# An adaptive-norm block on one core: load order, first stage, two orders in the step, and the second norm's statistics on ACT

## What is computed

```python
mod = silu(c) @ wmod                      # six rows of 128 per batch: sa, ca, ga, sb, cb, gb
ga, gb = sign(g) * max(|g|, 0.25)         # gates
h = layernorm(x) * (1 + ca) + sa
x = x + ga * attention(h)                 # eight heads of 16; windows of 64 tokens
h = layernorm(x) * (1 + cb) + sb          # the second norm
x = x + gb * ffn(h)                       # h + sum over 8 experts, two of them chosen by h[:, 0]
```

## Time and profile before

| | us |
|---|---|
| median of 3 runs | 681.24 |
| lowest and highest of them | 678.41, 683.61 |
| the profiled execution | 681.11 |
| its span, first to last instruction | 679.1 |
| mean granted clock of PE, share of full speed | 0.992 |

### The profile page before, as it was taken

How to read it: one execution, slowest core, us unless ns; L and a number is a source line. 1 busy time by engine, 2 the same in 40 slices (tenths; PEclk the granted TensorE clock), 3 DMA queues, 4 the chain that set the end, 5 groups by cost and what they waited for, 6 DMA issues and landing times. The chain is left out here.

```text
span 679.1 us, 22873 instructions
## 1 busy us (share of the span) xinstructions
PE 611.4 (90%) x6166; PEld 434.0 (64%) x6166; DVE 589.1 (87%) x4900; ACT 514.4 (76%) x1574; POOL 444.5 (65%) x723
## 2 busy tenths in 40 slices
PE   3989898999999999999999999999999999999886
PEld 2544456667666776666666766676666666776554
DVE  4885679999899989999999999999999899989860
ACT  2897257877888778877888888778888888778652
POOL 3011337778677767777777777777787677767651
PEclk9999899999999999999999999999999999999899
DMA  6220000000000000000110000000010000001000
GB/s 212 80 79 5 15 19 20 23 23 27 26 28 27 26 25 27 26 25 23 27 27 28 25 27 27 27 23 25 25 28 27 26 26 28 26 22 29 13 13 16
DMA packets 41183, 21.23 MB, mean 31 GB/s; under 512 B 6040, under 2 KB 40544, under 8 KB 41056
## 3 DMA queue, kind: packets, MB, share of 16 engines
q1 hardware_dynamic: 41056, 19.77, 10.2%
HBM read 10.45 MB, written 4.19 MB: 22 GB/s over the span
## 5 line engine op out<-in xcount | busy, mean ns | idle before, releaser
L1003 DVE MAX8 top<-modn_all 128x8 f32<-128x32 f32 x2048 | 208.1, 178 | 6.8 <-DVE meet L1095 0.5
L1009 DVE MATCH_REPLACE8 modn_all<-top,modn_all 128x32 f32<-128x32 f32 x1024 | 166.8, 176 | 0.0
L516 POOL TENSOR_TENSOR wmod_sb<-key,meet 128x512 f32<-128x512 f32 x64 | 67.7, 1058 | 114.7 <-DVE meet L1095 114.7
L1009 DVE MATCH_VALUE_LOAD modn_all<-top,modn_all 128x8 f32 x1024 | 80.8, 79 | 0.0
L1260 PEld LDWEIGHTS psC<-vst,big 128*128 128x128 f32 x512 | 62.0, 191 | 17.5 <-issue 17.5
L787 ACT ACTIVATE psD<-key 128x256 f32<-128x256 f32 x64 | 24.9, 389 | 62.3 <-issue 60.9
L1260 PE MATMUL psC<-vst,big 128*128 128x68 f32 x512 | 70.8, 280 | 0.0
L587 POOL TENSOR_TENSOR big<-big,con 128x512 f32<-128x512 f32 x64 | 69.8, 1091 | 0.7 <-DVE big L1064 0.7
L1260 PE MATMUL psC<-vdif,big 128*128 128x68 f32 x512 | 67.6, 274 | 0.0
L1260 PEld LDWEIGHTS psC<-vdif,big 128*128 128x128 f32 x512 | 62.3, 192 | 0.0
L1281 PE MATMUL psW<-con,wmod_sb 128*128 128x128 f32 x256 | 42.0, 287 | 19.3 <-POOL wmod_sb L516 19.3
(11 more groups left out here) (216 smaller groups left out, 1615.3 us busy)
## 6 DMA issues: line engine op xcount, KB each, us to landing
tst<-qT_all SPq DMA_DIRECT2D x256, 17.0 KB
big<-in_x SPq DMA_DIRECT2D x16, 256.0 KB, 2.9
xs<-in_x SPq DMA_DIRECT2D x64, 64.0 KB, 1.9
out<-yo SPq DMA_DIRECT2D x64, 64.0 KB, 1.6
sst<-nst SPq DMA_DIRECT2D x128, 3.0 KB
tst<-nst SPq DMA_DIRECT2D x128, 2.0 KB
con<-in_consts SPq DMA_DIRECT2D x1, 582.5 KB, 6.9
wmod_sb<-in_wmod SPq DMA_DIRECT2D x1, 384.0 KB, 5.8
```

The source lines that it names most:

```text
L516: nc.gpsimd.tensor_tensor(diff.rearrange("p (h j) -> p h j", h=NH), key[:, k % 2].rearrange("p (h j) -> p h j", h=NH), meet[:, k % 2, :, N ...
L1003: last = v.max(top[:, u, h, where], low_high[:, u, h])
L1009: last = v.match_replace(low_high[:, u, h], top[:, u, h, 1:9], low_high[:, u, h], GONE)
```

## The change

1. *Loads.* SP issues c first, then the identity alone (a DMA of its own), tile 0, wmod, tile 1, the query weights, the rest of the constants, tiles 2 and 3. Waits are split to match.
2. *First stage.* DVE clears a tile `warm`, on which PE makes 14 matmuls before it has work. The silu goes ahead of the first tile's statistics, tile 0 is normalised ahead of mod's two additions. The rows of mod, the Hebbian tables and the gate sizes leave the place ahead of the loop and stand within it: at n = 4 to 6 on ACT, n = 5 to 7 on PE, n = 10 on DVE.
3. *Routing.* PE makes the logits in step -2 and not -3, with other numbers of clock matmuls. DVE's last ten instructions of the expert gates go behind d2 of chunk 0. ACT's logarithm, root and influence of chunk 0 go behind the outer distances of chunk 1.
4. *The step, PE.* The masks go ahead of the counts.
5. *The step, ACT.* The root goes behind the copy L803, and the influence still stands last.
6. *The second norm.* bn_stats and bn_aggr leave DVE, and the three small instructions leave the head of ACT's step. ACT takes the sum with the copy to x2 (an accumulator), negates and scales it to the mean, squares x2 minus the mean with a second sum, and makes logarithm and exponential of that, all behind the copy and ahead of hi.

The diff, cut to its core (moved blocks that stay as they were are shown by their first lines):

```diff
@@ sync
-            for n in range(2):
-                sync.dma_start(xp[:, n], xh[:, n]).then_inc(xp_in[n], 16)
             sync.dma_start(c_sb[:], cin).then_inc(c_in, 16)
-            sync.dma_start(wmod_sb[:], wmod).then_inc(c_in, 16)
-            sync.dma_start(con[:], consts).then_inc(con_in, 16)
+            sync.dma_start(ident, consts[:, C_ID:C_ID + P]).then_inc(ident_in, 16)
+            sync.dma_start(xp[:, 0], xh[:, 0]).then_inc(xp_in[0], 16)
+            sync.dma_start(wmod_sb[:], wmod).then_inc(wmod_in, 16)
+            sync.dma_start(xp[:, 1], xh[:, 1]).then_inc(xp_in[1], 16)
             sync.dma_start(encq_sb[:], encq).then_inc(wq_in, 16)
+            sync.dma_start(con[:, C_MASK:C_END], consts[:, C_MASK:C_END]).then_inc(con_in, 16)
             for n in range(2, 4):
@@ scalar, first stage
-            act.wait_ge(c_in, 32)
+            act.wait_ge(c_in, 16)
...
-            act.wait_ge(pmod_ready, 2)
-            for j in range(2):
-                nc.scalar.activation(modn[:, j * 384:(j + 1) * 384], psW[0:NB, j, 0:384], ACT.Copy).then_inc(modn_ready, 1)
             act.wait_ge(modT_ready, 2)
             act.wait_ge(con_in, 16)
+            def modulation(j):
+                act.wait_ge(pmod_ready, 2 + j)
+                nc.scalar.activation(modn[:, j * 384:(j + 1) * 384], psC[0:NB, 0:384], ACT.Copy).then_inc(modn_ready, 1)
+            def hebbian():
+                act.wait_ge(pheb_ready, 2)
...
             to_hT(0, 0)
-            act.wait_ge(pheb_ready, 2)
...
                     to_q(n0 + u, u)
+                    if n0 == 4 and u < 2:
+                        modulation(u)
+                    if n0 == 4 and u == 2:
+                        hebbian()
@@ scalar, steps
+            def logarithm(k):
+                act.wait_ge(xT_ready, k + 1)
+                need(act, w_ready, k - 1)
+                if k == 0:
+                    act.wait_ge(r0_pe, 3)
+                nc.scalar.activation(infl[:, k % 2], pXT, ACT.Ln, bias=bias[:, 1:2]).then_inc(ln_done, 1)
+            def root(k):
...
+                nc.scalar.activation(e, e, ACT.Exp, scale=0.5).then_inc(root_done, 1)
+            def influence(k):
...
+                nc.scalar.activation(e, e, ACT.Exp, scale=-1.0).then_inc(infl_ready, 1)
             def step(i):
-                k = i - 4
-                if there(k):
-                    s = k % 2
-                    act.wait_ge(mvc_ready, k + 1)
...
-                    nc.scalar.activation(lv_c[:], mv_c[:, s, 1:2], ACT.Ln, bias=bias[:, 0:1]).then_inc(lnc_done, 1)
-                    nc.scalar.activation(nm_c[:, s:s + 1], mv_c[:, s, 0:1], ACT.Copy, scale=-1.0).then_inc(nm_done, 1)
-                    act.wait_ge(lnc_done, k + 1)
-                    nc.scalar.activation(rs_c[:, s:s + 1], lv_c[:], ACT.Exp, scale=-0.5).then_inc(rs_done, 1)
...
                     nc.scalar.activation(key[:, k % 2].rearrange("p (h j) -> p h j", h=NH), pA, ACT.Relu).then_inc(outer_ready, 1)
+                    if k == 1:
+                        logarithm(0)
+                        root(0)
+                        influence(0)
...
                 k = i - 3
                 if there(k):
+                    s = k % 2
                     act.wait_ge(att_ready, k + 1)
                     need(act, y_ready, k - 1)
-                    nc.scalar.activation(x2[:, k % 2], pAtt, ACT.Copy).then_inc(x2_ready, 1)
+                    need(act, rs_done, k)
+                    nc.scalar.activation(x2[:, s], pAtt, ACT.Copy, accum_out=sum_c[:]).then_inc(x2_ready, 1)
+                    act.wait_ge(x2_ready, k + 1)
+                    nc.scalar.activation(nm_c[:, s:s + 1], sum_c[:], ACT.Copy, scale=-1.0 / D).then_inc(nm_done, 1)
+                    act.wait_ge(nm_done, k + 1)
+                    nc.scalar.activation(dev_c[:], x2[:, s], ACT.Square, bias=nm_c[:, s:s + 1],
+                                         accum_out=ssq_c[:]).then_inc(ssq_done, 1)
+                    act.wait_ge(ssq_done, k + 1)
+                    nc.scalar.activation(lv_c[:], ssq_c[:], ACT.Ln, bias=bias[:, 0:1], scale=1.0 / D).then_inc(lnc_done, 1)
+                    act.wait_ge(lnc_done, k + 1)
+                    nc.scalar.activation(rs_c[:, s:s + 1], lv_c[:], ACT.Exp, scale=-0.5).then_inc(rs_done, 1)
                 k = i + 1
                 if there(k):
...
                     nc.scalar.activation(pHi, high, ACT.Copy, scale=-1.0).then_inc(hi_ready, 1)
-                    e = infl[:, k % 2]
...
-                    nc.scalar.activation(e, e, ACT.Exp, scale=0.5).then_inc(root_done, 1)
+                    if k:
+                        logarithm(k)
                 if there(i):
...
                     nc.scalar.activation(pHigh, top[:, 1].rearrange("p h n -> p (h n)"), ACT.Copy,
                                          scale=-1.0).then_inc(high_done, 1)
+                k = i + 1
+                if there(k) and k:
+                    root(k)
...
-                if there(k):
-                    e = infl[:, k % 2]
-                    act.wait_ge(root_done, k + 1)
-                    nc.scalar.activation(e, e, ACT.Exp, scale=-1.0).then_inc(infl_ready, 1)
+                if there(k) and k:
+                    influence(k)
@@ vector
-            stats(0, 0)
+            v.memset(warm[:], 0.0).then_inc(warm_set, 1)
             dve.wait_ge(ec_ready, 1)
...
+            stats(0, 0)
             stats(1, 1)
+            normalise(0, 0)
             dve.wait_ge(modT_ready, 1)
...
-            normalise(0, 0)
             normalise(1, 1)
...
-            dve.wait_ge(modn_ready, 2)
-            gview = modn.rearrange("b (u v d) -> b u v d", u=2, v=3)[:, :, 2]
...
+                    if n == 10:
+                        gate_sizes()
...
+            def expert_gates():
+                link(v.tensor_reduce(s8[:, 16, 0:1], s8[:, 12], AX_X, ALU.add))
...
                     v.scalar_tensor_tensor(out=e, in0=pB, scalar=0.0, in1=e, op0=ALU.max, op1=ALU.min).then_inc(d2_ready, 1)
+                    if k == 0:
+                        expert_gates()
...
-                k = i - 3
-                if there(k):
-                    dve.wait_ge(x2_ready, k + 1)
-                    need(dve, mvc_ready, k)
-                    v.bn_stats(st_c[:], x2[:, k % 2]).then_inc(stc_ready, 1)
...
-                    v.bn_aggr(mv_c[:, k % 2], st_c[:]).then_inc(mvc_ready, 1)
@@ tensor
+            pe.wait_ge(warm_set, 1)
+            for n in range(14):
+                mm(psC[0:1, :], warm[:, 0:1], warm[:], start=True, stop=True)
             pe.wait_ge(sil_ready, 1)
+            pe.wait_ge(wmod_in, 16)
...
-            for j in range(2):
-                last = mm(psW[0:NB, j, 0:384], sil[:], wmod_sb[:, j * 384:(j + 1) * 384], start=True, stop=True)
-            last.then_inc(pmod_ready, 1)
-            pe.wait_ge(con_in, 16)
-            pe.wait_ge(wq_in, 16)
-            pe.wait_ge(modn_ready, 2)
+            pe.wait_ge(ident_in, 16)
...
+                    if n0 == 5 and u < 2:
+                        modulation(u)
+                    if n0 == 5 and u == 2:
+                        hebbian()
...
                     need(pe, n2_ready, k - 1)
+                    need(pe, nst_ready, k)
...
                 if i == -3:
                     routing_front()
-                    keep_clock(psC, PW, 6)
+                    keep_clock(psC, PW, 8)
+                if i == -2:
                     routing_logits()
-                if i == -2:
-                    keep_clock(psC, PW, 8)
+                    keep_clock(psC, PW, 4)
...
+                k = i + 2
+                if there(k):
+                    need(pe, d2_ready, k)
+                    if k == 1:
+                        pe.wait_ge(pair_done, 2)
+                    for r in range(NR):
+                        masks(r)
                 drained({NCH - 1: 3, NCH: 3}.get(i, 0))
                 k = i - 1
                 if there(k):
                     pe.wait_ge(f_ready, 2 * k + 2)
...
                     pe.wait_ge(rows_in[k % 2], ROWS_IN * (k // 2) + ROWS_IN)
-                    need(pe, d2_ready, k)
-                    if k == 1:
-                        pe.wait_ge(pair_done, 2)
-                    for r in range(NR):
-                        masks(r)
                     last = distances(k % 2)
```

More of the change, by code:

```diff
@@ L858, in every_8th, with gate_sizes @@
                                 AX_X, ALU.add).then_inc(qsum8_ready, 1)
-            stats(0, 0)
+            def gate_sizes():
+                dve.wait_ge(modn_ready, 2)
+                gview = modn.rearrange("b (u v d) -> b u v d", u=2, v=3)[:, :, 2]
+                link(v.tensor_scalar(gsgn, gview, 0.0, 2.0, ALU.is_ge, ALU.mult))
+                link(v.tensor_scalar(gabs, gview, -1.0, None, ALU.mult))
+                link(v.tensor_tensor(gabs, gabs, gview, ALU.max))
+                link(v.tensor_scalar(gabs, gabs, 0.25, None, ALU.max))
```

(21 more changed lines are left out.)

76 lines of the change are left out of this document (41 added, 35 removed).

## The result

The changed kernel takes 695.23 us (median of 4 runs, 690.37 to 696.91) beside 680.50 for the kernel before on the same chip, so it is 14.7 us slower by the medians; the ratio of the means is 1.020, 95% interval 1.0135 to 1.0267. The forecast was 689, "same" or "slower" at equal chances. The profiled execution took 694.36 with a span of 692.5, 13.4 longer than before.

| stretch | before | after | measured | forecast |
|---|---|---|---|---|
| start to first scan | 92.52 | 98.81 | +6.29 | -2.6 |
| first scan to the scan of chunk 2 | 17.24 | 16.85 | -0.39 | -0.3 |
| 58 steps, chunk 2 to chunk 60 | 517.72 | 526.98 | +9.26 | +11.2 |
| last three steps | 27.84 | 27.08 | -0.76 | +0.9 |
| behind the last scan | 23.76 | 22.76 | -1.00 | -1.5 |

What follows compares the result with a forecast made beforehand. A ring of waits through DVE, POOL, PE and ACT, no single full engine, bounded the kernel. Terms 11.2 - 0.3 + 0.9 - 1.6 - 1.0 - 1.5 = +7.7 on 681.24 gave 689 us, range 677 to 701.

Steps and rivals of the forecast that it cites:

- +11.2: The 58 steps from chunk 2 to chunk 60: 528.9 us instead of 517.72, with plain steps of 9.03 instead of 8.63.
- -1.6: Loads and first stage: earlier third normalisation gains 2.9, moved gate sizes take back about 1.3; bounds -4 to +1.5.
- the forecast's own branch: Case where the step's ring of waits runs through masks and ACT's statistics: 683 to 695 us, chance 0.50.
- The chain: ACT's five dependent statistics activations between x2 and its negated copy: 1.56 us, bounds 1.25 to 1.92.
- The masks fill no gap: PE in each step: masks start only when d2 ends, so counts and all behind them move 0.68 later.
- the 1.5 expected: Tail behind the last scan: shorter x2 to n_c saves 1.0, the last chunk 0.5, so -1.5 us.
- Routing -1.0: Routing before the first scan: later expert gates gain some 0.4, the late root 0.6; bounds -2.5 to +0.5.
- The last three: +0.9: Last three steps: 0.9 us longer, including +0.4 for each of the two that contain ACT's negated copy.
- rival 3: Steps: ACT's statistics take 1.92, or PE's clock drops; 711 us, with half of it 700; chance 0.15.
- The scan still waits for L803, by about 0.9: Sign of being right, in a plain step: DVE's scan still waits about 0.9 us for ACT's copy.
- rival 2: Steps: DVE was the limit, so a step falls to 7.92 at best; 634 us, with half 657; chance 0.10.
- the 8.37 behind the late root: Plain step with the root moved later: 8.37 instead of 8.63, without DVE's idle 0.26, DVE then the limit.

Runs made afterwards that it cites:

- u_stats: Changed kernel with the second norm's statistics back on DVE, masks still ahead and root late: 662.52 us, ratio 0.972.
- best_dve: u_stats_ins plus the 14 clock matmuls of a_fill: 653.41 us, ratio 0.957.
- best_split: Front of u_stats_ins, clock matmuls of a_fill, and masks and statistics placed as in u_masks_split: 650.86 us, ratio 0.953.
- b_rm: Kernel before with masks ahead of the counts and root behind the copy L803, statistics on DVE: 655.78 us, ratio 0.963.
- b_root: Kernel before with only the root moved behind the copy L803: 662.27 us, ratio 0.970.
- b_masks: Kernel before with only the masks moved ahead of the counts: 683.97 us, ratio 1.006.
- u_stats_ins: u_stats with mod's rows, Hebbian tables and gate sizes put back ahead of the first stage's loop: 655.48 us, ratio 0.960.
- u_steps: Changed kernel with masks, root and second-norm statistics put back as before, leaving new loads, first stage and routing: 685.86 us, ratio 1.0043.
- a_fill: Changed kernel with 14 more PE clock matmuls in step -1, ahead of the turn of the expert gates: 692.75 us, ratio 1.014.
- u_masks: Changed kernel with only the masks put back behind the attention's product: 664.51 us, ratio 0.974.
- b_stats: Kernel before with only the second norm's statistics moved to ACT: 702.99 us (two runs), ratio 1.031.
- u_masks_split: u_masks with the logarithm and exponential of the variance moved behind ACT's copy to pHigh: 660.16 us, ratio 0.968.

## Why the prediction was right and wrong

*The time and the direction.* 689 was 6 below the median, inside the range. The steady state was the right part of it: its mechanism held, and its +11.2 came out as +9.26. The start of the kernel did not: its two terms, -1.6 and -1.0, came out as +3.7 and +2.5, both outside their own bounds (+1.5 and +0.5 at most). So the whole was +13.4 in the traces where +7.7 was forecast, and 695.23 lies just above the 683 to 695 of the forecast's own branch. That it fell into the range is luck in part: the range reached to 701 for a dearer chain, and the chain was not dearer. What was right by its own steps:

- The chain. Forecast 1.56 from x2 to hi, measured 341.38 - 339.80 = 1.58 and 1.59, 1.60 in two other kernels. The square took 0.40 where 0.36 was taken; the two read-outs ended 0.08 and 0.10 behind their instruction (0.09), the waits were 0.03 to 0.04.
- The masks fill no gap: they start at DVE's end of d2 and put the attention's product back by 0.60 (forecast 0.68). That 0.08, less 0.03 in the chain and behind hi, made the plain step 8.99 and not 9.04. The longer steps came at 9.18, 9.18 and 9.38, forecast 9.17, 9.23 and 9.43.
- n_c of a last chunk follows x2 by 683.57 - 681.73 = 1.84, forecast 1.7; the time behind the last scan fell by 1.0 of the 1.5 expected.

```profile
681.73 0.27 ACT L808 ACTIVATE x<-psX 128x128 f32<-128x128 f32 x1
...
683.57 0.45 POOL L545 TENSOR_SCALAR n_c<-x,nm_c,rs_c 128x128 f32<-128x128 f32 x1 [0.64 <-ACT rs_c L817]
```

What failed:

- **"PE's modulation and Hebbian products, now in the loop too, have PE's slack there."** They haven't where they stand: PE runs there without idle time, a tile in 2.15. And each insertion makes ACT wait for a product that PE makes behind the tile's queries, and PE then waits for the tile that ACT scales behind its copy. I counted instructions on PE and asked who waits for them on no engine. The insertions cost 5.0, and the term "-1.6" was +3.5 over the groups above (+3.7 in the two traces).
- **"Routing -1.0."** The term lacked the clock altogether, which I had allowed only as a rival's reason in the steps. From the end of the first stage to the first scan the kernels took, by the mean granted clock of that stretch:

  | mean granted clock | old routing | new routing |
  |---|---|---|
  | 1.00 | | 30.78 (u_stats, best_dve, best_split) |
  | 0.95 | 32.36 (b_rm), 32.39 (b_root), 32.64 (b_masks) | 32.36 (u_stats_ins), 33.01 (u_steps) |
  | 0.90 | 33.87 (before) | 33.41 (a_fill), 33.77 (u_masks) |
  | 0.85 | 35.26 (b_stats) | |
  | 0.81 | | 36.41 (changed), 36.43 (u_masks_split) |

  The time goes with the clock, and at an equal clock the two orders take about the same: b_rm and u_stats_ins, which have the same step, both 32.36. So the new order was worth nothing that these traces show, and the +2.5 is the lower clock of this trace, 0.81 beside 0.90. Why it was lower stays open.
- **"The last three: +0.9."** They took 0.76 less, but this mixes in the clock. In the kernel before it fell there (a mean of 0.83 in the step of 10.20 that begins at 636.76), in the changed one it did not. So my remark in rival 3, that nothing of a lower clock shows in the longer steps of before, was wrong too: the longest of them has it.
- **"The scan still waits for L803, by about 0.9."** It waits for nothing. I left out the pairs, which stand between hi and the scan on DVE: hi's end, 0.04, two pairs of 0.4 and the scan take as long as hi, the logarithm and the copy on ACT. The sum was right (hi to scan 1.19, forecast 1.18) because the two ways tie.
- **The floor of rival 2, 7.92, and the 8.37 behind the late root.** With statistics on DVE the step without waits is 8.28; without them single steps of 8.02 are the lowest seen (the third and fourth of u_masks_split). So the statistics cost DVE some 0.26 a step, not the 0.45 that their durations sum to: neighbours on DVE overlap (in the rows of u_stats the aggregate starts at 321.03, lasts 0.16, and the pairs start at 321.12), as I had counted on ACT but not here. The mechanism was right that DVE sat waiting: taking 0.26 from it could not help while ACT was late.

The rule of the Trainium skill that I had weighed ("Perfetto Trace Analysis", section "Optimizing Scalar/DVE Operations": offload to Scalar if DVE is saturated) can now be set beside runs. In the kernel before DVE was not saturated, and the offload cost 21.3 in 58 steps (some 15.7 without the excess of the three slow ones). With the root late DVE is, since a plain step waits for nothing (b_root, b_rm). There the whole chain ahead of hi gained 1.9 with the masks behind (501.79 to 499.88), but cost 32.6 with the masks ahead (494.36 to 526.98). Half of it behind the copy gained 6.6 more, which leaves 493.28, only some 1 below what the kernels with statistics on DVE, masks ahead and root late take (494.11 to 494.36). So a saturated DVE was not enough here: what the offload was worth hung on its place in ACT's queue and on what else stood ahead of hi.

## What to carry to other kernels

Before work is moved to an idler engine, look at what stands behind its new place in that engine's queue and who waits for that; a share of busy time answers neither, and half a microsecond ahead of or behind one instruction was worth 6.6 us in 58 steps. Try the parts of a change in pairs as well as singly: the same reordering of PE cost 2.9, gained 7.4 or cost 27.1 us depending on the other two parts. And an insertion into a pipelined loop should not make two engines wait for each other in one turn. Here taking the insertions out of the loop gained 5.0; letting their product be taken a turn later than it is made was not tried.

## What the runs showed of the hardware

The granted clock of PE fell to half, 1.2 GHz, in one trace and stayed at full, 2.4 GHz, in another behind the same wait (2.43 and 2.44); in a third, with that wait filled, it fell before the wait was reached. The stretch to the first scan took 30.78 at the full clock and up to 36.43 at a mean of 0.81. Four executions of one kernel (u_stats) took from 656.28 to 666.00 at mean clocks from 0.986 down to 0.972. The clock also fell within three steps of the kernel with the statistics on ACT alone (a mean of 0.70, 0.70 and 0.84 in steps of 11.28, 11.35 and 10.42), while the changed kernel, with plain steps of 8.99 beside 9.07, shows none; no run shows why. A sum taken with an activation of 128x128 is read out by an instruction of 0.19 to 0.20 us, of which only 0.08 to 0.10 shows in the queue.
